# A two-layer transformer kernel: the transfers of the negated maxima are issued by ScalarE instead of SyncE, with a new order table

## What is computed

```
h = layernorm(x) * (1 + ca) + sa
qkv = einsum('bsd,ed->bse', h, w_qkv)     # 16 heads of 8
q, k = rope(q, k)
scores = einsum('bhqd,bhkd->bhqk', q, k)  # 512 x 512 per head
probs = softmax(scores, axis=-1)
out = einsum('bhqk,bhkd->bhqd', probs, v)
x = x + ga * (out @ w_out.T)
```

## Time and profile before

| | |
|---|---|
| median of 3 runs | 1085.66 us (1082.01 to 1087.82) |
| the profiled execution | 1092.12 us, of which span 1089.9 us |
| mean granted TensorE clock | 0.93 |
| PE, DVE, ACT, POOL busy | 926.0, 776.2, 655.6, 426.8 us |
| transfers issued by SyncE for the maxima | 64 of 6 KB |

### The profile page before, as it was taken

The page is one execution under the profiler, slowest core; times in us unless marked ns, Lnnn a source line. Parts: engine busy times, 40 slices in busy tenths (PEclk is TensorE's granted clock), DMA queues, the critical chain, the costliest instruction groups (busy, mean ns, idle before and its releaser), DMA issues. The chain is left out here.

```text
span 1089.9 us, 15616 instructions
## 1 busy us (share of the span) xinstructions
PE 926.0 (85%) x5176; PEld 513.5 (47%) x5176; DVE 776.2 (71%) x1467; ACT 655.6 (60%) x1176; POOL 426.8 (39%) x537
## 2 busy tenths in 40 slices
PE   4247678997899799998999998999998999889785
PEld 2111135443444355554554654446464466368553
DVE  6566678677756877788867777888878765546665
ACT  1236664666656758668768576866856756745441
POOL 2161042226112815574134364653556244454300
PEclk9558988999999989999999999999999899979876
DMA  8520304001300140111300014150001000010010
GB/s 233 154 66 30 60 30 98 33 1 55 59 2 1 32 101 9 34 43 58 62 1 13 16 61 86 59 105 11 1 25 33 2 21 16 20 35 1 18 34 10
DMA packets 54536, 47.09 MB, mean 43 GB/s; under 512 B 12393, under 2 KB 50025, under 8 KB 53114
## 3 DMA queue, kind: packets, MB, share of 16 engines
q1 hardware_dynamic: 53898, 45.85, 16.7%
q10 hardware_dynamic: 560, 0.26, 0.1%
HBM read 30.97 MB, written 14.73 MB: 42 GB/s over the span
## 5 line engine op out<-in xcount | busy, mean ns | idle before, releaser
L1557 DVE TENSOR_REDUCE negmax<-scores_for_max 128x2 f32<-128x1024 f32 x252 | 307.9, 1222 | 73.7 <-PE scores_for_max L932 71.3
L1269 ACT ACTIVATE probs<-scores 128x1024 f32<-128x1024 f32 x256 | 262.0, 1023 | 91.8 <-PE scores L956 90.7
L1030 PE MATMUL shared_ab<-eo,mu 128*128 128x128 f32 x1024 | 143.4, 283 | 9.0 <-ACT scaled L1383 4.8
L1030 PEld LDWEIGHTS shared_ab<-eo,mu 128*128 128x128 f32 x1024 | 129.0, 193 | 45.2 <-issue 28.1
L966 PE MATMUL weighted_values<-probs,vaug 128*32 128x512 f32 x1024 | 142.3, 630 | 1.0 <-ACT probs L1269 0.9
L1953 POOL TENSOR_TENSOR acc<-acc,scaled 128x512 f32<-128x512 f32 x55 | 71.2, 1294 | 178.8 <-ACT scaled L1383 178.7
L1692 DVE SCALAR_TENSOR_TENSOR mu<-th,expert_units 128x512 f32<-128x512 f32 x112 | 76.7, 685 | 72.4 <-ACT th L1311 71.6
L932 PE MATMUL scores_for_max<-ks,qs 48*128 48x512 bf16 x504 | 102.6, 404 | 27.8 <-DVE negmax L1557 19.4
L572 PE MATMUL expert_units<-hb_hi,e_lo 128*128 128x512 f32 x224 | 112.2, 501 | 15.3 <-DVE mu L1692 9.7
L956 PE MATMUL scores<-qs,ks 51*128 51x512 bf16 x512 | 102.2, 396 | 20.8 <-ACT probs L1269 17.7
L1311 ACT ACTIVATE th<-expert_units 128x512 f32<-128x512 f32 x112 | 66.8, 597 | 78.8 <-PE expert_units L574 77.2
(11 more groups left out here) (320 smaller groups left out, 1590.8 us busy)
## 6 DMA issues: line engine op xcount, KB each, us to landing
parts_d<-parts SPq DMA_DIRECT2D x15, 384.0 KB, 2.5
qs<-parts_d SPq DMA_DIRECT2D x14, 384.0 KB, 6.1
ks<-parts_d SPq DMA_DIRECT2D x14, 384.0 KB, 9.8
w<-in_L_ffn_w SPq DMA_DIRECT2D x16, 256.0 KB, 3.9
parts_d<-parts SPq DMA_DIRECT2D x15, 256.0 KB, 2.7
xp<-in_L_attn_x SPq DMA_DIRECT2D x8, 256.0 KB, 3.0
probs<-in_L_ffn_w_kernel SPq DMA_DIRECT2D x2, 1024.0 KB, 7.7
x<-in_L_attn_x SPq DMA_DIRECT2D x8, 256.0 KB, 2.9
```

Of the source, the lines that this page charges most:

```text
L1030: last = nc.tensor.matmul(m0[:, at], mu[:, (2 * e + f) % 4, at], eo[:, e, f, :], start=(f == 0), stop=(f == HALVES - 1))
L1269: nc.scalar.activation(probs[:, kt % 2, j, :, :].rearrange("p m s -> p (m s)"), se[:, :], ACT.Exp)\
L1557: V.tensor_reduce(negmax[:, g % 2, :, n], max_bank(b, g, n)[:, :].rearrange("p (m s) -> p m s", m=2), AX, ALU.max, negate=True)\
```

## The change

ScalarE issues the two transfers of a group right behind its copy, after a wait for this copy; SyncE has no `mrow` step any more. The semaphores and the transfers themselves are the same. The table `SLOTS` is a new one for all engines; the sets of steps of the others are unchanged, their order is not. A part of TensorE's second column step gets one further wait, for VectorE's two columns of the first layer.

```diff
@@ SLOTS (all 237 lines renewed; the step moved)
-    ("A", "mrow"): dict(sp=(37, 39, 41, 43, 44, 46, 51, 53, 54, 58, 60, 62, 63, 65, 67, 72, 76, 82, 84, 86, 88, 90,
-        91, 96, 103, 106, 110, 113, 116, 119, 122, 125), act=(47, 60, 79, 91, 103, 127, 149, 172, 189, 202, 212, 233,
-        256, 280, 307, 325, 380, 394, 420, 440, 463, 489, 502, 541, 581, 595, 622, 651, 684, 698, 724, 764)),
+    ("A", "mrow"): dict(act=(55, 66, 78, 87, 100, 123, 145, 170, 189, 203, 214, 232, 256, 280, 305, 325, 379, 395,
+        420, 440, 463, 489, 501, 541, 580, 595, 622, 653, 684, 698, 725, 762)),
...
-            def mrow_out(b, g):
-
-                after_all(sp, ("a_mrow", b, g + 1))
-                for m in range(2):
-                    at = HALF * m + STACK
-                    sp.dma_start(qs[at:at + PARTS, b % 2, GP * g:GP * (g + 1), :]
-                                 .rearrange("n p (t s) -> n (p t) s", s=P),
-                                 mrow[8 * PARTS * m:8 * PARTS * (m + 1), :]).then_inc(sig["a_row"], 16)
...
-                      ("A", "load"): a_load, ("A", "mrow"): mrow_out,
+                      ("A", "load"): a_load,
...
                     if L:
                         pe.wait_ge(s_cr, 16 * N_CONST)
+                        pe.wait_ge(s_cols, 2)
...
                 nc.scalar.activation(mrow[:, :], m0[0:PARTS * 16, 0:P // 2].bitcast(bf16), ACT.Copy)\
                     .then_inc(sig["a_mrow"], 1)
+                after(act, "a_mrow", b, g + 1)
+                for m in range(2):
+                    at = HALF * m + STACK
+                    nc.scalar.dma_start(qs[at:at + PARTS, b % 2, GP * g:GP * (g + 1), :]
+                                        .rearrange("n p (t s) -> n (p t) s", s=P),
+                                        mrow[8 * PARTS * m:8 * PARTS * (m + 1), :]).then_inc(sig["a_row"], 16)
```

More of the change, by code:

```diff
@@ new lines @@
+    ("A", "onorm"): dict(dve=(235, 244, 251, 261, 285, 321, 338, 351, 376, 399, 414, 433, 457, 488, 508, 536, 576,
+        580, 605, 619, 637, 677, 710, 727, 756, 778, 808, 836, 860, 903, 920, 932)),
+    ("A", "load"): dict(sp=(19, 40, 48, 53, 67, 72, 82, 91)),
+    ("A", "vcopy"): dict(pool=(15, 34, 63, 82, 125, 146, 186, 217)),
+    ("A", "wog"): dict(dve=(217, 350, 429, 514, 598, 708, 767, 877)),
+    ("B", "load"): dict(sp=(15, 46, 51, 61, 68, 79, 89, 96)),
+    ("B", "oT"): dict(pe=(168, 320, 474, 633, 786, 944, 1109, 1256)),
@@ new lines @@
+    ("B", "x2"): dict(pool=(62, 86, 123, 149, 187, 216, 241, 242), dve=(2, 29, 30, 31, 43, 44, 93, 994)),
+    ("C", "load"): dict(sp=(39, 56, 63, 76, 85, 90, 95, 100)),
+    ("C", "loadu"): dict(sp=(37, 58, 69, 78, 86, 92, 98, 101)),
+    ("C", "loadd"): dict(sp=(28, 60, 73, 81, 88, 94, 99, 102)),
+    ("C", "stats"): dict(dve=(354, 436, 544, 629, 740, 838, 930, 995)),
+    ("C", "rstd"): dict(pool=(66, 102, 127, 155, 197, 218, 243, 268)),
+    ("C", "xn"): dict(act=(201, 326, 400, 550, 631, 699, 796, 817), dve=(18, 19, 20, 61, 65, 66, 68, 997)),
@@ L253 @@
+    ("C", "sim"): dict(pe=(526, 637, 874, 1002, 1111, 1216, 1298, 1335)),
+    ("C", "simmax"): dict(dve=(469, 542, 685, 768, 840, 911, 974, 1015)),
     ("C", "simexp"): dict(act=(316, 393, 540, 624, 694, 765, 832, 863)),
[L254 to L257 removed]
@@ L298 @@
-    ("P", "modpe"): dict(pe=(41, 42, 48, 58, 184, 213, 221, 356)),
-    ("P", "raw"): dict(sp=(2, 3, 4, 5, 7, 8, 9, 13)),
-    ("P", "late"): dict(sp=(6, 10, 11, 12, 14, 16, 17, 24)),
+    ("C", "simsum"): dict(dve=(472, 545, 689, 771, 843, 913, 977, 1017)),
+    ("C", "out"): dict(pe=(538, 647, 887, 1012, 1117, 1228, 1306, 1337)),
+    ("C", "res"): dict(dve=(476, 547, 691, 774, 845, 917, 980, 1019)),
+    ("C", "stats3"): dict(dve=(479, 554, 692, 775, 849, 919, 981, 1020)),
+    ("C", "rstd3"): dict(pool=(107, 132, 170, 199, 223, 238, 262, 272)),
@@ new lines @@
+    ("C", "dn"): dict(pe=(599, 601, 812, 819, 953, 958, 1065, 1067, 1170, 1172, 1258, 1259, 1326, 1328, 1343, 1344)),
+    ("C", "fin"): dict(dve=(517, 520, 646, 649, 735, 738, 809, 811, 883, 885, 938, 939, 1006, 1011, 1031, 1032)),
+    ("C", "outp"): dict(sp=(59, 71, 80, 87, 93, 97, 103, 104)),
+    ("C", "keep"): dict(pool=(81, 114, 143, 183, 204, 228, 251, 253), dve=(15, 26, 63, 64, 84, 99, 112, 1018)),
+    ("C", "keep3"): dict(pool=(108, 150, 184, 206, 224, 244, 267, 270), dve=(45, 46, 49, 100, 101, 102, 128, 1022)),
@@ new lines @@
+    ("C", "w2g"): dict(pool=(33, 142, 180, 195, 212, 237, 265, 271)),
+    ("P", "e0hi"): dict(act=(19, 20, 27, 28, 29, 31, 40, 49)),
+    ("P", "e1hi"): dict(act=(21, 30, 32, 33, 34, 47, 94, 97)),
+    ("P", "whhi"): dict(act=(16, 23, 24, 25, 26, 37, 38, 53)),
+    ("P", "small"): dict(act=(63, 67, 73, 77, 114, 117, 155, 156)),
+    ("P", "e1lo"): dict(pool=(7, 10, 11, 12, 19, 22, 23, 37)),
+    ("P", "mod1"): dict(dve=(131, 254, 258, 271, 277, 280, 282, 303)),
+    ("P", "whlo"): dict(dve=(180, 184, 195, 197, 208, 211, 212, 214)),
@@ new lines @@
+    ("P", "e0lo"): dict(dve=(179, 188, 191, 204, 215, 220, 225, 234)),
+    ("P", "modst"): dict(sp=(10, 11, 12, 13, 14, 16, 21, 23)),
+    ("B", "downd"): dict(dve=(7, 8, 9, 10, 11, 12, 13, 14, 16, 27, 28, 47, 48, 136, 990, 992)),
+    ("B", "gsum"): dict(dve=(1, 3, 4, 5, 6, 50, 67, 989)),
+    ("C", "row"): dict(pe=(1, 2, 3, 4, 5, 19, 24, 1255)),
+    ("C", "upb"): dict(pe=(7, 8, 9, 10, 11, 12, 13, 14, 15, 16, 26, 33, 34, 44, 1333, 1336)),
+    ("C", "out0"): dict(pe=(6, 17, 18, 28, 38, 45, 48, 1331)),
@@ L301 @@
+    ("P", "modpe"): dict(pe=(46, 47, 52, 53, 328, 380, 449, 498)),
+    ("P", "raw"): dict(sp=(2, 3, 5, 6, 8, 9, 18, 20)),
+    ("P", "late"): dict(sp=(4, 25, 26, 29, 30, 32, 35, 42)),
 }
```

229 lines of the change are left out of this document (94 added, 135 removed), and 176 rows, old and new, of the table SLOTS.

## The result

The changed kernel takes 1122.62 us (median of three runs, 1121.67 to 1125.78) where the kernel before took 1085.66. The ratio is 1.035, with a 95% interval of 1.031 to 1.039: 37 us slower. The forecast was slower by 12 us, and its range ended at 1120, so the sign came out right and the size did not.

What follows compares the result with a forecast made beforehand. It took TensorE, 92% busy mid-run and trading one scores bank with ScalarE, as the bound. Terms -2 + 17 - 3 + 0 gave +12 us: about 1104 us profiled, 1098 us median, range 1076 to 1120 us.

Steps and rivals of the forecast that it cites:

- (1), (2): Removed hop from ScalarE's copy to SyncE (0.03 us) and SyncE's late starts (18 us in 6 groups); 2 us gain.
- (3): SyncE saves 45 us of issue time and its other loads no longer queue behind copies; taken as 0.
- (4): ScalarE waits for its copy and issues two transfers, 32 times; 1.75 us a pair, between 1.47 and 2.05.
- (5): Pair time not covered by ScalarE's gaps behind the 32 copies: 22, 29 or 35 us at 1.5, 1.75 or 2.0 us.
- (6): Share of ScalarE's delay that reaches TensorE and the run time: 60% of 29, 17 us; bounds 7 to 35.
- (7): Transfer latency in batch 0's exposed groups grows up to 0.6 us each, 3 us at most, inside the other bounds.
- New table: New order of all engines' steps, much the same pipeline; 3 us recovered, between 10 us gain and 5 us loss.
- Head: Stretch from 0 to 138 us: first projection some 5 us later, mostly covered; 3 us later to 4 earlier, taken 0.
- C: Full price: slower ScalarE issues and coupled banks pass on half to two thirds, 25 to 40 us, 1111 to 1126; 10%.
- A: Absorbed: the pair sits in ScalarE's idle time and the table routes TensorE around it; 0, 1086 us; 23%.
- B: Faster: freed SyncE and the new table decide, little of ScalarE's delay reaches TensorE; -9 us, 1077 us; 22%.
- D: No stall, since ScalarE issues while its array works on something else; same time as A and counted in its chance.

Runs made afterwards that it cites:

- old_table_pad5: Kernel before, SyncE still issuing all transfers, with five useless chained ScalarE copies added behind each copy of the maxima; 1124.15 us, ratio 1.0351.
- act_batch0_only: Kernel before with its old order table, ScalarE issuing only the 8 transfers of batch 0 and SyncE the other 56; 1097.29 us.
- old_table_act: Kernel before with its old order table, only the issue of both transfers moved from SyncE to ScalarE behind its copy; 1123.93 us, ratio 1.0342.
- new_table_sp: Changed kernel's new order table, but SyncE issues the pairs again, at places set by the copies' times; 1105.02 us, ratio 1.0165 to the kernel before.

## Why the prediction was right or wrong

- **Bound of the kernel.** Right in that all that holds ScalarE up costs (`old_table_pad5`), and the waits that grew are the named ones. That it is the scores bank in particular was not tried: the two waits of the round trip grew by 11 and 13 us, but VectorE's for the tanh grew by 16 (75.3 to 91.5).
- **(1), (2) the hop and SyncE's lag, -2 us.** Nothing was gained: 4.3 us of wait for rows instead of 4.7. In the trace before SyncE was over 1 us late in 5 groups, 15.7 us in all, not in 6 with 18 us.
- **(3) SyncE freed, 0 us.** The wrong sign was not thought of. SyncE ran ahead and put its loads in front of the rows, 4.3 us of wait in one group of `act_batch0_only` and 3.4 in `old_table_act`. The kernel after has only 1.7 us there, and so has `new_table_sp`, in which SyncE issues.
- **(4) the pair, 1.75 us.** 1.48 to 1.51 us, the lower end. The middle was a poor choice between two rows; the row for the same transfer on another engine was the nearer one.
- **(5) the missing time, 22, 29 or 35 us.** This step failed first. The idea was right and the reading wrong: in 11 groups I skipped the instruction that had started before the copy's end. From the same trace the sums are 34.7, 41.4 and 48.2 us, and the trace of `old_table_act` shows 37.8.
- **(6) 60% of it reaches the time.** This step failed as well, and it weighs more. `old_table_act` lost 37 us (32 to 42) for 34.7 uncovered: 107%, where 60% would give 21. So nothing of what ScalarE stood longer was won back in sum. The upper bound of 100% was nearly right, and with the right sum it would have held the result: 48 us. I took a delay for something that can only be lost on the way; the table of delays shows it kept for hundreds of us. In batch 0 it also grew: four stalls, 5.0 us in the trace, made 17 us by 1.1, with TensorE's same matmuls 11.5 us slower at the lower clock and 4.3 us of wait for the rows. The sum had no term for a longer busy time of TensorE (+9 us in one execution).
- **(7) latency, up to 3 us in batch 0.** Too little: all that the change does in batch 0 costs 12 us (6 to 17).
- **New table, -3 us (10 gain to 5 loss).** Beside ScalarE's issues it changed nothing (1.035 and 1.0342), inside the bounds. By itself it costs 18 us, which I had not seen. I had named a shift of the tail by over 5 us as a sign of being wrong; it shifted by 7.1 (179.8 against 172.7 us behind the last copy).
- **Head, 0.** The first exponential stands at 80.06 us instead of 80.38, with the first stack loaded at 51.34 instead of 43.93. That is 7.4 us later where I had worked out 5, and it was covered as expected.
- **The rivals.** C, full price, was what happened, with the lower end of its pair and a larger share: 37 of the 32 x 1.5 = 48 us. It had 10%, and the part of it above 1120 us lay outside the range. A, B and D are out; the stall was there in all 32 groups.

## What to carry to other kernels

A transfer issued by a compute engine costs that engine the issue and the wait ahead of it. Line up each such stall with the idle time at its own place in the order. What is not covered is the cost: here a pair cost about as much as ScalarE really stood longer, a stall half as long cost less than that, and one twice as long more. In reading the idle times, take the next instruction of the order and not the next start behind the end: an instruction that follows at once starts before the one ahead has ended, and who skips it finds idle time where there is none. When a queue is relieved of a wait, look at which large transfers will now start earlier and what small, urgent one they will pass.

## What the runs showed of the hardware that I had not expected

An issue of the same 6 KB takes 0.705 us on SyncE, 0.720 us on ScalarE and 0.58 us on POOL, though a 128 x 128 load took 0.60 us on ScalarE and 0.43 on SyncE. Scores waited 4.3 and 6.5 us for 12 KB of rows issued some 4.6 us behind the first of loads of 1.5 MB. Instructions of ScalarE that follow at once overlap by 0.10 us (108.38 against 108.48). And a delay of 17 us made in batch 0 was kept within 0.2 us over almost 200 us of fixed order.
